# A drain behind every four gathers on GpSimd in a four-layer graph network

## The reference

```python
x = _layernorm(x + _L0_gnn_ref(x, edge_weight, src, dst))          # weighted sum of x[src]
x = _layernorm(x + _L1_gnn_ref(x, edge_index, ...))                # attention over xl[src] + xr[dst]
x = _layernorm(x + _L2_gnn_ref(x, edge_index, edge_attr_64, ...))  # two-layer MLP on each edge
x = _layernorm(x + _L3_gnn_ref(x, src, dst, ...))                  # mean of x[src], gated mix
```

## Time and profile before

| | us |
|---|---|
| timed runs, median of 3 | 4491.54 |
| lowest and highest | 4491.3, 4494.27 |
| profiled execution, first to last instruction | 6105.3 |
| GpSimd busy in it | 3211.4 (53%) |
| TensorE matmul, weight load | 3148.5 (52%), 2593.6 (42%) |
| VectorE, ScalarE | 2498.6 (41%), 968.1 (16%) |
| mean granted TensorE clock | 0.688 |

### The profile page before, as it was taken

One profiled execution on the slowest core, in us unless ns is written; L12 is line 12 of the kernel. 1 busy time (PEld: TensorE's weight loads), 2 busy tenths in 40 slices (PEclk: granted clock), 3 DMA queues, 4 the chain that ended last, 5 costly groups with the idle time before them and its releaser, 6 DMA issues.

```text
span 6105.3 us, 52726 instructions
## 1 busy us (share of the span) xinstructions
PE 3148.5 (52%) x17147; PEld 2593.6 (42%) x17150; DVE 2498.6 (41%) x4988; ACT 968.1 (16%) x2133; POOL 3211.4 (53%) x3332
## 2 busy tenths in 40 slices
PE   3443444436656566565535565565567334433336
PEld 2333333335545455454424555455556323323324
DVE  5554555634433334333533333333334522322228
ACT  0000000122211112111111111111111301111115
POOL 6666666364544444444364544444443366666662
PEclk8555555677777777777757777777778655666557
DMA  3141111134444444444233333333333211111112
GB/s 87 45 134 44 46 46 46 45 94 123 127 117 122 114 124 120 117 122 111 71 95 97 98 100 97 93 101 93 100 98 84 69 47 46 44 46 45 46 45 70
DMA packets 601180, 514.20 MB, mean 84 GB/s; under 512 B 99694, under 2 KB 532781, under 8 KB 600910
## 3 DMA queue, kind: packets, MB, share of 16 engines
q0 software_dynamic: 105248, 216.15, 13.9%
q10 hardware_dynamic: 210704, 154.61, 9.6%
q1 hardware_dynamic: 284958, 140.08, 8.4%
HBM read 410.93 MB, written 91.26 MB: 82 GB/s over the span
## 4 chain that ended last, share of the span: by engine, by line
another core or an unknown queue 37%; PE 24%; DVE 16%; issue 13%; ACT 5%; ACTq 2%; DVEq 1%; POOL 1%; DMA 1%; SPq 0%; POOLq 0%
PE bank L690 22%; DVE acc L1504 4%; DVE work L1542 3%; PE bank L695 2%; DVE bank L1527 2%; DVE quads L1517 1%; ACT acc L1092 1%; DVE quads L1529 1%; DVEq L375 1%; ACTq L1126 1%; ACT quads L1251 1%; ACTq L1121 1%; ACT quads L1219 1%; ACTq L1129 0%
## 5 line engine op out<-in xcount | busy, mean ns | idle before, releaser
L690 PE MATMUL bank<-quads,work 128*128 128x128 f32 x3920 | 656.2, 313 | 919.5 <-issue 589.3
L690 PEld LDWEIGHTS bank<-quads,work 128*128 128x128 f32 x3920 | 599.3, 223 | 1078.1 <-issue 731.7
L1504 DVE TENSOR_TENSOR acc<-bank,acc 128x512 f32 x588 | 403.2, 686 | 1323.2 <-remote 1063.4
L1100 ACT COPY bank<-zeros 128x384 f32<-128x384 f32 x588 | 283.4, 483 | 2104.6 <-DVE acc L1504 1423.0
L582 POOL DMA_INDIRECT g<-xl,srct x392 | 377.2, 962 | 450.4 <-DVE msg L1828 332.4
L582 POOL DMA_INDIRECT g<-a_src,srct x392 | 377.6, 963 | 442.6 <-PE bank L690 324.6
L582 POOL DMA_INDIRECT nodes<-xl,srct x390 | 374.1, 959 | 380.5 <-DVE msg L1828 265.3
L582 POOL DMA_INDIRECT nodes<-a_src,srct x390 | 374.1, 959 | 358.1 <-PE bank L690 232.7
L1913 DVE TENSOR_TENSOR msg<-bank,b_b 128x512 f32<-128x512 f32 x196 | 135.6, 692 | 994.9 <-PE bank L690 557.5
L582 POOL DMA_INDIRECT g<-x,srct x392 | 371.2, 947 | 240.7 <-issue 116.4
L690 PE MATMUL bank<-quads,g 128*128 128x128 f32 x1568 | 351.9, 393 | 282.7 <-issue 182.1
(11 more groups left out here) (377 smaller groups left out, 6082.1 us busy)
## 6 DMA issues: line engine op xcount, KB each, us to landing
partial<-acc ACTq DMA_DIRECT2D x196, 288.0 KB
work<-local_rank ACTq DMA_DIRECT2D x392, 128.0 KB
work<-xr_by_rank SPq DMA_DIRECT2D x784, 64.0 KB
work<-b_by_rank SPq DMA_DIRECT2D x784, 64.0 KB
work<-in_rel_t ACTq DMA_DIRECT2D x196, 128.0 KB
g<-acc SPq DMA_DIRECT2D x126, 64.0 KB, 1.9
g<-in_x,srct POOLq DMA_INDIRECT x392
scan_penalties<-work SPq DMA_DIRECT2D x14, 448.0 KB
```

The source lines that it names most:

```text
L690: return nc.tensor.matmul(to, lhsT, rhs, start=start, stop=stop, skip_group_check=True)
L1100: nc.scalar.copy(partial_bank(l, i)[:, P:QE].rearrange("p (t e) -> p t e", e=P), zeros[:, 0:P].unsqueeze(1).broadcast_to([P, TQ - 1, P])). ...
L1504: v.tensor_tensor(window, partial_bank(l, q)[:, :], window, ALU.add).then_inc(partial_copied, 1)
```

## The change

GpSimd gets one drain behind the gathers of each quad, in all four layers: 196 drains a layer, 784 in all. The drain stands at L586 of the changed kernel, and what follows it in the file moves down by a line. Nothing else is added, removed or moved.

```diff
@@ -583,6 +583,7 @@
                             quad_rows(l, i)[:, t, :], None, table,
                             bass.IndirectOffsetOnAxis(srct[:, i * TQ + t:i * TQ + t + 1].bitcast(U32), 0),
                         ).then_inc(gathered[i % RING], 16)
+                    pool.drain()
 
             def chain():
```

## The result

| | before | after |
|---|---|---|
| timed runs, median of 4, us | 4492.91 | 6686.62 |
| lowest and highest, us | 4491.3, 4495.21 | 6677.07, 6688.4 |
| profiled execution, first to last instruction, us | 4496.2 (a second one) | 6685.8 |
| GpSimd busy | 72% | 48% |

The ratio is 1.487, with an interval of 1.4852 to 1.4887. The 784 drains cost 2194 us, 2.80 us each; the forecast was 0.50 us each and 4884 us, and the result lies far above its range. The profiled execution shown ahead of the prediction was a disturbed one, so the kernel before was profiled once more (e0_before_again, one run of 4497.95 us), and what follows compares with that.

A forecast was written before the change was run, and what follows sets the result against it. The prediction took GpSimd's gathers to pace all four sweeps. Each drain's 0.05 us plus a 0.75 us restart, in place of a 0.30 us gap, adds 0.50 us; 784 make 392 us on 4491.5, 4884 us, range 4580 to 5285 us.

The forecast's parts named there:

- The bound: All four layers: GpSimd's gathers, one every 1.25 us and 5.00 us a quad, pace the timed runs.
- The sum: Kernel before: 3128 gathers at 1.251 us plus the time outside the gather stretches, less shorter lags, give 4534 us.
- Layers 1 and 2 hide it: Rival: GpSimd has time to spare in layers 1 and 2, only layers 0 and 3 pay; +196 us, 4688 us; chance 0.13.
- A cheap drain: Rival: GpSimd restarts behind a drain as quickly as behind the select, 0.13 us more each; 4593 us; chance 0.05.
- Not slower: the consumers pace: Rival: consumers pace the sweeps and GpSimd's waiting time absorbs the drains; time stays at 4491 us; chance 0.09.
- The drain does nothing: Rival: each drain is through as soon as the sequencer reaches it, hidden by run-ahead; 4491 us; chance 0.03.
- The run-ahead term: Behind each quad's drain: the next gather starts after 0.75 us without run-ahead, where gathers now follow at 0.30 us.
- The drain's own cost: Behind each quad's gathers: the drain takes 0.05 us beyond the work it waits for.
- My step from it: Drain behind gathers: as the record ends with the descriptors, a drain needn't wait for the landing; the cost stays 0.50 us.
- The drain waits for the landing: Rival: 1.76 us of landing precedes each 0.75 us restart, +2.21 us a quad, +1733 us, 6224 us; chance 0.08.

The follow-up runs named there:

- e0_before_again: The kernel before, unchanged, profiled once more: one run of 4497.95 us.
- e3_fill: Changed kernel with each drain replaced by an unused iota behind the gathers of 764 of 784 quads, waited for only later: 4598.96 us, ratio 1.022.
- e2_no_run_ahead: Changed kernel with each drain replaced by a one-column memset and a wait for that memset alone, not for any transfer: 5022.9 us, ratio 1.1155.
- e1_wait_landing: Changed kernel with each drain replaced by a wait for the count of the quad's own gathers, that is their landing: 6563.63 us, ratio 1.4577.
- e5_drain_2: Changed kernel with its drains limited to layer 2, 196 drains in all: 5269.08 us, ratio 1.1734.
- e7_wait_previous: Changed kernel with each drain replaced by a wait for the landing of the quad before: 4506.66 us, ratio 1.0028.

## Why the prediction was wrong

**The bound** was right, and so was its reading of the disturbed profile. The second profile spans 4496.2 us with the longest wait of L1504 down from 30.1 us to 11.7; e3_fill charges full price in all layers. The sum came to 4534 us by two errors that offset each other: the stretches are 3953 us where I had 3913, and 543 us lie outside where I had 621. That the total was within 1% is thus in part luck. The rival *Layers 1 and 2 hide it* is dead: they pay 2.72 and 3.99 us a quad, more than the others. *A cheap drain* (4593 us), *Not slower: the consumers pace* and *The drain does nothing* fall with the result, and e2_no_run_ahead shows that the restart alone costs more than they allow.

**The run-ahead term** was right in kind. e2_no_run_ahead shows 0.66 us a quad where the working has 0.50, and 0.11 of the 0.66 are its memset.

**The drain's own cost is the step that failed**: "so I count 0.05 us for the drain". In its place stood the landing and what the drain settles, 1.8 us behind the last record in the quiet layers and 3.7 us in layer 2. The 0.05 came from the drain between two selects, whose work is over when its record is. A gather's is not. The row to weigh was the first drain of L654, the only one of the seven with gathers in front of it, and only one select between: 22.143 us long and 7.85 us of gap. I offered two readings, "one more late count of the profiled execution, or an effect of the gathers in front", and let the median of the seven decide, six of which have no gathers in front. The same place in the second profile of the kernel before, which has no late counts:

```profile
4353.97 2.55 POOL L653 TENSOR_SCALAR out<-work,iota_col 128x896 f32<-128x896 bf16 x1
4364.36 2.08 POOL L655 TENSOR_TENSOR out<-out,msg 128x896 f32<-128x896 f32 x1 [7.85 <-issue]
```

and in the changed kernel, whose gathers had been drained:

```profile
6551.36 2.53 POOL L654 TENSOR_SCALAR out<-work,iota_col 128x896 f32<-128x896 bf16 x1 [2.59 <-issue]
6554.05 2.15 POOL L656 TENSOR_TENSOR out<-out,msg 128x896 f32<-128x896 f32 x1 [0.16 <-issue]
```

and in e1_wait_landing, where every gather had been waited for but none drained:

```profile
6421.42 2.53 POOL L655 TENSOR_SCALAR out<-work,iota_col 128x896 f32<-128x896 bf16 x1 [2.55 <-DMA work<-x,srct]
6431.80 2.07 POOL L657 TENSOR_TENSOR out<-out,msg 128x896 f32<-128x896 f32 x1 [7.85 <-issue]
```

7.85 us to the hundredth in three executions of two kernels, and 0.16 us where the gathers had been drained before: it was an effect of the gathers, and one that a wait for their landing doesn't take away. The 0.03 us start of the select, which I held against the landing, says nothing of a drain, since no drain stood between those two.

**The rule** of the Trainium skill's page "Perfetto Trace Analysis", section on the DMA instruction of GpSimd, that its record ends with the descriptors and not with the data, agrees with the trace: the rows of a quad come 1.57 us after the record in layer 0 and 3.84 us after it in one quad of layer 2. My step from it was false. A record that ends early tells when the engine is free, and not what a drain waits for. The rule of the Trainium skill's page "GPSIMD Engine Reference", section 2.1 (Instruction dispatch), that consecutive instructions are no barrier between the cores, is worth little here: e2_no_run_ahead waits for an instruction of GpSimd that stands behind the gathers, so whatever it costs that GpSimd's own work must be over lies within its 0.66 us a quad, of 2.80. How much of the 0.66 that is, no run shows.

**The rival *The drain waits for the landing*** had the mechanism and, for two layers, the price: 2.21 us a quad, measured 2.34 and 2.18 in layers 0 and 3. Its 6224 us is 463 us short because I took the landing of a quiet layer, 1.76 us, for all. Even its price in the quiet layers was met by two errors that offset each other: the landing there is 1.6 us, and the drain's own 0.20 us behind it was left out. Layer 1's surcharge is (2.72 - 2.21) x 196 = 100 us and layer 2's (3.99 - 2.21) x 196 = 349 us, which is nearly all of the difference. In layer 1 more than half of the quads land as early as in a quiet layer (median 1.72 us, mean 2.17), in layer 2 nearly all land late (3.53 and 3.44). The rival had 0.08 where the row of 22 us should have made it a leading case, and the range left it out. That row, though, showed only that a drain behind gathers is dear: its 7.85 us stay in e1_wait_landing, where everything had landed, and so are no measure of the landing.

**The sum as the runs give it**: no run-ahead 520 us (e2_no_run_ahead), the landing 2061 - 520 = 1541 us (e1_wait_landing less that), the drain's settling beyond the landing 133 us (the rest; 123 us by the two medians); together 2194 us. With the memset's 86 us taken out of the first term and put to the second, they are 434 and 1627 us. The profiled span, for which I expected 0 to 250 us, grew by 580 us over the one shown and by 2190 us over the second: late counts came with that one execution and not with the profiler, as every later profile shows.

**What stays open.** Why the drain takes longer the more gathers lie behind the last one, why the growth seems to stop at 64, and why it is 7.85 us behind a select (6.53 us in e5_drain_2, whose last drain lay 782 gathers back), no run shows. Nor was it tried which of the loads in layer 2 meet a quad's transfers so regularly, while in layer 1, at more bytes a second (125 against 87 GB/s), the surcharge is less than a third of layer 2's. No version here is faster than the kernel before.

## What to carry to other kernels

Before a drain or a wait goes behind a DMA, ask whether the data must be there at that point: a drain on GpSimd behind gathers costs the landing under the traffic of that stage, plus the restart of an engine that had run ahead. Where the order of an older transfer is enough, wait on its count, as e7_wait_previous does for 0.3%; that says nothing of the newest. And a single odd row with the right instruction in front of it is worth more than the median of six rows without.

## What the hardware showed that I had not expected

- A drain on GpSimd holds until the indirect transfers issued before it have landed: 775 of 784 drains ended 0.20 us after the last count of their quad, with a landing of 1.58 us (median) in layer 0 and 3.53 us in layer 2.
- Beyond the landing a drain has a part that grows with the gathers since the last one, 0.041 us each up to 32, for a gap of 6.08 us from 64 to 256 gathers in layers 2 and 3 and of 6.65 to 7.14 us in layer 1; and 7.85 us behind a select after all 3128.
- Loads on the queues of SyncE and ScalarE lengthen the landing of GpSimd's gathers although the DMA engines were busy only 0.35 of the time: 3.99 us a quad in place of 2.2, and back to 2.3 when both loads were small (0.18 busy).
- An iota of 0.25 us between two gathers costs 0.12 us, as the gap behind it is shorter than that between two gathers.
